# Expert products of a vision tower contracted over 128 + 64 rows instead of 96 + 96

## The reference

```python
# L0_ffn: W1 is 8 x 192 x 1024, W2 is 8 x 512 x 192
h = jnp.einsum('ecd,edh->ech', xg, W1)
act = h[..., :H] * jax.nn.silu(h[..., H:])
ye = jnp.einsum('ech,ehd->ecd', act, W2)
...
# L2_ffn: Wg and Wu are 16 x 768 x 192, Wd is 16 x 192 x 768
gate = jax.nn.silu(jnp.einsum('ecd,efd->ecf', xg, Wg))
up = jnp.einsum('ecd,efd->ecf', xg, Wu)
out = jnp.einsum('ecf,edf->ecd', gate * up, Wd)
```

## Time and profile before

| | us |
|---|---|
| median of 3 runs | 1151.77 |
| lowest, highest | 1146.94, 1162.23 |
| profiled execution | 1161.12 |
| span in its profile | 1159.3 |
| PE busy, share of the span | 77% |
| PE weight loads busy | 66% |
| DVE, ACT, POOL busy | 46%, 29%, 23% |

### The profile page before, as it was taken

The page is one execution under the profiler, slowest core; times in us unless marked ns, Lnnn a source line. Parts: engine busy times, 40 slices in busy tenths (PEclk is TensorE's granted clock), DMA queues, the critical chain, the costliest instruction groups (busy, mean ns, idle before and its releaser), DMA issues. The chain is left out here.

```text
span 1159.3 us, 31081 instructions
## 1 busy us (share of the span) xinstructions
PE 896.2 (77%) x13412; PEld 761.6 (66%) x13412; DVE 528.1 (46%) x1168; ACT 332.3 (29%) x677; POOL 261.9 (23%) x289
## 2 busy tenths in 40 slices
PE   8889986998369906899856795777779999387594
PEld 5578863886369905778755673655479999265472
DVE  1469963445343155554423365462821111464464
ACT  0247732212112202442442232333101212133132
POOL 1169840330134323210100101111033322200100
PEclk9989997778579967898876697785969999588598
DMA  7168757400458020000005100000438991100000
GB/s 211 29 142 184 177 154 227 102 1 1 136 168 222 23 63 1 2 3 1 2 1 139 47 4 1 2 3 27 124 83 208 259 222 14 30 3 1 2 4 23
DMA packets 58450, 88.29 MB, mean 76 GB/s; under 512 B 10756, under 2 KB 45000, under 8 KB 58340
## 3 DMA queue, kind: packets, MB, share of 16 engines
q1 hardware_dynamic: 53220, 81.85, 26.7%
q0 software_dynamic: 5120, 4.88, 2.2%
HBM read 78.30 MB, written 7.30 MB: 74 GB/s over the span
## 5 line engine op out<-in xcount | busy, mean ns | idle before, releaser
L2647 DVE TENSOR_TENSOR L_ffnhid<-L_ffnact_gate,L_ffnbank_u 128x300 f32<-128x300 f32 x32 | 15.0, 468 | 118.9 <-ACT L_ffnact_gate L2666 112.4
L1810 POOL TENSOR_SCALAR stage_hat_x<-stage_hat_x 128x320 f32<-128x320 f32 x40 | 51.2, 1280 | 20.4 <-ACT stage_hat_x L1786 20.4
L1720 PE MATMUL ps_places<-stage_own_y,stage_spread 80*64 80x128 f32 x800 | 54.8, 285 | 0.0
L1870 DVE TENSOR_TENSOR stage_product<-ps_rows,stage_hat_x 128x960 f32<-128x960 f32 x40 | 46.3, 1158 | 18.5 <-PE ps_rows L1731 15.2
L1731 PE MATMUL ps_rows<-stage_strip,stage_hat_y 64*32 64x96 f32 x3200 | 49.8, 256 | 6.3 <-DMA stage_strip<-in_strips 3.2
L1731 PEld LDWEIGHTS ps_rows<-stage_strip,stage_hat_y 64*32 64x32 f32 x3200 | 40.6, 108 | 13.4 <-issue 13.4
L1720 PEld LDWEIGHTS ps_places<-stage_own_y,stage_spread 80*64 80x64 f32 x800 | 44.9, 142 | 6.2 <-issue 0.8
L1110 PE MATMUL L_attnbank_q<-L_attnhT,L_attnwq 128*128 128x200 f32 x192 | 42.7, 369 | 6.9 <-DVE L_attnqT L1275 6.7
L2580 POOL DMA_INDIRECT stage_y_rows<-L_ffndown,stage_choice_index x16 | 25.4, 1589 | 90.4 <-ACT L_ffndown L2673 57.0
L1875 DVE TENSOR_REDUCE stage_samples<-stage_product 128x120 f32<-128x960 f32 x40 | 45.7, 1144 | 0.0
L1818 POOL TENSOR_TENSOR stage_hat_x<-stage_rel_x,stage_w_column 128x160 f32<-128x160 f32 x80 | 35.2, 461 | 45.8 <-POOLq L1522 45.8
(11 more groups left out here) (427 smaller groups left out, 2227.5 us busy)
## 6 DMA issues: line engine op xcount, KB each, us to landing
stage_strip<-in_strips SPq DMA_DIRECT2D x80, 189.0 KB, 3.6
L_ffn_win<-in_L_ffn_Win SPq DMA_DIRECT2D x10, 1152.0 KB
stage_L_ffn_win<-in_L_ffn_Win SPq DMA_DIRECT2D x6, 1152.0 KB
L_ffnranks<-stage_ranks SPq DMA_DIRECT2D x16, 400.0 KB
L_ffn_win<-in_L_ffn_Win SPq DMA_DIRECT2D x8, 768.0 KB
L_ffn_wout<-in_L_ffn_Wout SPq DMA_DIRECT2D x10, 576.0 KB
stage_L_ffn_wout<-in_L_ffn_Wout SPq DMA_DIRECT2D x6, 576.0 KB
L_ffn_wout<-in_L_ffn_W SPq DMA_DIRECT2D x8, 384.0 KB
```

Source lines behind the costliest of these rows:

```text
L1720: mm = nc.tensor.matmul(ps_places[HALF_P * h:HALF_P * (h + 1), p % 2, g * P:(g + 1) * P], k.spread[:, p * GRID + g, :], places[:, h * P:(h ...
L1810: nc.gpsimd.tensor_scalar(x, x, 1.0, 1.0, ALU.min, ALU.subtract).then_inc(s["hat_x"], 1)
L1870: nc.vector.tensor_tensor(products(i % 2), in_psum(i % 2), weights_x(i % BUFFERS), ALU.mult).then_inc(s["multiplied"], 1)
```

## The change

Channels are no longer split 96 + 96 but 128 + 64 (`REST` = 64). For each index tile f, gate and up are each one matmul over channels 0 to 127, and then one over channels 128 to 191. The rests of gate and up use different halves of PE's rows: gate rows 0 to 63, up rows 64 to 127. For this `win` gets a third block of columns, in which partitions 0 to 63 hold gate's last 64 channels and partitions 64 to 127 up's, laid out on the host; and `xT` holds the last 64 channels of the tokens twice, on both halves of the partitions. `turn` makes the second copy with a plain matmul by the identity whose output stands on partitions 64 to 127. The number of matmuls of `up` is the same, as is the order of its blocks; what `win` holds is as many bytes as before. Nothing else is changed.

```diff
-        xT = sb("xT", [HALF, 2, HALVES, 2 * C])
+        xT = sb("xT", [P, 2, 2, 2 * C])
...
-        ps_x = bank_x[0:HALF, :, 0:HALVES * 2 * C].rearrange("q b (k c) -> q b k c", k=HALVES)
+        ps_x = bank_x[:, :, 0:2 * 2 * C].rearrange("q b (k c) -> q b k c", k=2)
...
-                for h in range(HALVES):
-                    for k in range(2):
-                        mm = nc.tensor.transpose(ps_x[:, e % 2, h, k * C:(k + 1) * C], x[0:C, e, k, h * HALF:(h + 1) * HALF], tw.identity[0:C, 0:C])
+                for k in range(2):
+                    own = slice(k * C, (k + 1) * C)
+                    nc.tensor.transpose(ps_x[:, e % 2, 0, own], x[0:C, e, k, 0:P], tw.identity[0:C, 0:C])
+                    nc.tensor.transpose(ps_x[0:REST, e % 2, 1, own], x[0:C, e, k, P:DIM], tw.identity[0:C, 0:C])
+                    mm = nc.tensor.matmul(ps_x[REST:P, e % 2, 1, own], x[0:C, e, k, P:DIM], tw.identity[0:C, 0:C], start=True, stop=True)
...
                 for f in range(fb):
-                    for ps, at in ((ps_g, 0), (ps_u, hidden)):
-                        o = at + (c * fb + f) * P
-                        for k in range(HALVES):
-                            mm = nc.tensor.matmul(ps[:, c, f, :], weights.win[e % NB][:, k, o:o + P], xT[:, e % 2, k, :], start=(k == 0), stop=(k == 1))
+                    mm = weights.project_in(nc.tensor, e, c * fb + f, xT[:, e % 2], ps_g[:, c, f, :], ps_u[:, c, f, :])
...
-            self.win.append(tw.sb(f"{self.name}_win{b}", [HALF, HALVES, 2 * self.hidden]))
+            self.win.append(tw.sb(f"{self.name}_win{b}", [P, 3 * self.hidden]))
...
-        sp.dma_start(self.win[b][:], self.w_in[e].rearrange("(k q) n -> q k n", q=HALF)).then_inc(self.loaded[b], 16)
+        sp.dma_start(self.win[b][:], self.w_in[e]).then_inc(self.loaded[b], 16)
...
+    def project_in(self, pe, e, f, xT, gate, up):
+        w = self.win[e % len(self.win)]
+        low, high = slice(0, REST), slice(REST, P)
+        for ps, at in ((gate, 0), (up, self.hidden)):
+            pe.matmul(ps, w[:, at + f * P:at + (f + 1) * P], xT[:, 0, :], start=True, stop=False)
+        rest = slice(2 * self.hidden + f * P, 2 * self.hidden + (f + 1) * P)
+        pe.matmul(gate, w[low, rest], xT[low, 1, :], start=False, stop=True)
+        return pe.matmul(up, w[high, rest], xT[high, 1, :], start=False, stop=True)
```

More of the change, by code:

```diff
@@ L24 @@
 HALF = DIM // HALVES
+REST = DIM - P
 GROUPS = HEADS // 4
@@ L2544, in experts_by_row @@
         x = sb("x", [C, n_exp, DIM])
-        xT = sb("xT", [HALF, 2, HALVES, C])
+        xT = sb("xT", [P, 2, 2, C])
         act_gate = sb("act_gate", [P, 2, fb, C])
@@ L2549, in experts_by_row @@
         bank_x, bank_g, bank_u, bank_d = pb("bank_x"), pb("bank_g"), pb("bank_u"), pb("bank_d")
-        ps_x = bank_x[0:HALF, :, 0:HALVES * C].rearrange("q b (k c) -> q b k c", k=HALVES)
+        ps_x = bank_x[:, :, 0:2 * C].rearrange("q b (k c) -> q b k c", k=2)
         ps_g, ps_u = (b[:, :, 0:fb * C].rearrange("p b (f c) -> p b f c", f=fb) for b in (bank_g, bank_u))
@@ L2598, in turn @@
                     pe.wait_ge(s["xT_ready"], e - 1)
-                for k in range(HALVES):
-                    mm = nc.tensor.transpose(ps_x[:, e % 2, k, :], x[:, e, k * HALF:(k + 1) * HALF], tw.identity[0:C, 0:C])
+                nc.tensor.transpose(ps_x[:, e % 2, 0, :], x[:, e, 0:P], tw.identity[0:C, 0:C])
+                nc.tensor.transpose(ps_x[0:REST, e % 2, 1, :], x[:, e, P:DIM], tw.identity[0:C, 0:C])
+                mm = nc.tensor.matmul(ps_x[REST:P, e % 2, 1, :], x[:, e, P:DIM], tw.identity[0:C, 0:C], start=True, stop=True)
                 mm.then_inc(s["x_in_psum"], 1)
@@ L3140, in layout, with gate_and_up @@
     o["L0_ffn_Wg"] = a["L0_ffn_Wg"]
-    o["L0_ffn_Win"] = np.concatenate([a["L0_ffn_W1"][..., h:], a["L0_ffn_W1"][..., :h]], 2)
+    def gate_and_up(gate, up):
+        rest = np.concatenate([gate[:, P:], up[:, P:]], 1)
+        return np.concatenate([gate[:, :P], up[:, :P], rest], 2)
+    o["L0_ffn_Win"] = gate_and_up(a["L0_ffn_W1"][..., h:], a["L0_ffn_W1"][..., :h])
     o["L0_ffn_W2"] = a["L0_ffn_W2"]
     o["L2_ffn_gate"] = a["L2_ffn_gate_weight"].T
-    o["L2_ffn_Win"] = np.concatenate([a["L2_ffn_Wg"].transpose(0, 2, 1), a["L2_ffn_Wu"].transpose(0, 2, 1)], 2)
+    o["L2_ffn_Win"] = gate_and_up(a["L2_ffn_Wg"].transpose(0, 2, 1), a["L2_ffn_Wu"].transpose(0, 2, 1))
     o["L2_ffn_Wout"] = a["L2_ffn_Wd"].transpose(0, 2, 1)
```

## The result

| | before | after |
|---|---|---|
| median, us | 1156.95 | 1182.35 |
| lowest, highest | 1146.94, 1162.23 (4 runs) | 1179.41, 1186.32 (4 runs) |
| profiled execution, its span | 1161.12, 1159.3 | 1179.41, 1177.6 |

The ratio is 1.0221, with a 95% interval of 1.016 to 1.0283: 25 us slower. The forecast was 1180 and +28. That the kernel is slower is clear of the noise; that it is slower by more than 2%, the line that the forecast drew, is not.

A forecast was written before the change was run, and what follows sets the result against it. PE was taken to bound both expert stretches; index tiles +12.3 (stage 6) and +0.1 (stage 2), token transposes +16.6 and half clock -0.7 gave +28 us, 1180 against a median of 1151.8. Range 1162 to 1214 us, own range 1168 to 1192.

The forecast's parts named there:

- the line that the forecast drew: About 2% from the time before, at 1174.8 us, within which a measurement is not told from no change.
- What bounds: Expert stretches of stages 2 and 6: PE alone limits, so each nanosecond its queue gains or loses goes into the time.
- Halves side by side: 64-row rests of gate and up run together, starts 0.007 us apart; rival that they take turns, 1214 us, 11%.
- The price of a change: Each PE shape switch: 0.20 us plus 0.845 ns per moving column, 0.284 in stage 6, 0.403 in stage 2; no-drain rival 6%.
- The transposes: Token blocks: +0.49 us an expert in stage 6, +1.10 in stage 2, 16.6 in all; smaller-drain rival, 1169 us, 8%.
- Half clock: First 20 us of stage 6 and half of stage 2's first 11: together -0.7 us; large clock-falls rival, 1275 us, 6%.
- What costs nothing: Weight layout, transfers and wider token copies in the expert stages: no added time, as weights run ahead and ACT is idle.
- Sum: Whole kernel: 12.3 + 0.1 + 16.6 - 0.7 = +28 us, giving 1180 us against the median 1151.8.

The follow-up runs named there:

- experiment 3: Changed kernel with both rests on the low 64 rows of PE (up's values not the reference's): 1247.81 us, ratio to before 1.0791.
- Experiment 4: Changed kernel with the order inside every other index tile reversed, rests first, so one change of shape per tile instead of two: 1160.92 us, ratio to before 1.0064.
- experiment 2: Changed kernel with both rests contracted over all 128 rows, token block unchanged (values not the reference's): 1174.36 us, ratio to before 1.0174.
- Experiment 1: Changed kernel with the tokens' second copy made by transposes alone, no plain matmul left in the token block: 1173.97 us, ratio to before 1.0173.
- experiment 6: Kernel before with only `win` loaded as in the changed one, PE reading 96 rows (values not the reference's): 1155.79 us, ratio 0.9977.
- experiment 7: Changed kernel with rests over all 128 rows and the second token copy by transposes (values not the reference's): 1150.77 us, ratio to before 0.9949.
- experiment 11: Kernel of experiment 7 made to compute the reference, with zeros on the other operand's half of the moving tokens: 1154.38 us, ratio to before 0.9971.
- experiment 12: Kernel of experiment 11 with the rests of gate and up done in one matmul into one PSUM bank: 1148.65 us, ratio to before 0.9892.
- experiment 5: Changed kernel with every other tile's order reversed and the second token copy made by transposes alone: 1149.95 us, ratio to before 0.9925.
- 8: Kernel of experiment 7, unedited, run again for a second profile: 1152.45 us, ratio to before 0.9935.

## Why the prediction was right

- *What bounds.* PE alone, in both stretches, as forecast: they grew by 24.9 us and the time by 25.4. That the two agree this well is in part luck, since the time outside the stretches differs by up to 14 us from one execution to the next.
- *Halves side by side.* Right: a low and a high record start 0.007 apart, as forecast (they stand as 0.00 or 0.01 above), and forcing them to take turns costs 0.21 us a tile (experiment 3).
- *The price of a change.* 0.20 us plus the last columns: the forecast tile of stage 6, 1.02, is 1.017; stage 2's 1.625 is 1.613. Experiment 4 takes out one change for a tile and gets back 0.172 in stage 6 (0.284 - 0.112, to the digit), experiment 2 both.
- The Trainium skill (TensorEngine Tiling (Array Packing), Key Properties) says that changing the tiling mode drains TensorE. The trace agrees, and shows what it is worth here: 0.28 us with 100 columns, as much as two and a half records of stage 6.
- *The transposes.* Forecast +0.49 and +1.10 us for an expert, measured +0.49 (0.583 from first transpose to gate in place of 0.175, and the gate's own load exposed, 0.08) and +1.04 (1.35 in place of 0.41, and 0.10 for the load). Experiment 1 shows that the plain matmul is the cause.
- *Half clock.* Unchanged at 20 us in stage 6, by the rows of both profiles; a tile there is 1.78 us (857.05 to 858.83 in the timeline), 1.79 forecast.
- *What costs nothing.* Layout and wider copies: right (experiment 6 for the layout; experiment 7, whose tile is 0.894 and whose PE waits for a copy once, 0.5 us, as before, for both). That the transfers got lighter I had not seen.
- *Sum.* 28 forecast, 25 measured. The terms by the trace: tiles 0.123 x 96 = 11.8 less 0.009 x 32 = 0.3, tokens 7.8 + 8.3, together 27.6 at full clock. In the stretches it was 24.9: each begins behind its first token block (1.5 us), and at half clock a tile of stage 6 loses only 0.07 (1.78 against 1.71), 0.6 us over the first eleven. The median of before was 1151.8 when I forecast and 1157 to 1159 in the later runs, so the 1180 fell 5 short by its base and 3 over by its sum. That it lies 2 us from the measured 1182.35 is these two errors in part cancelling; the sum itself is right to a tenth.

## What to carry to other kernels

Count a switch between PE tile shapes as a lost weight load and an emptied pipe, here 0.28 us at 100 columns and full clock, and order the matmuls so that two groups of the same shape stand next to each other; look for it in the weight loads, since the matmul records show PE busy throughout. A transpose with a narrow output was free of it here, a plain matmul on the same tile was not. Where a half-empty contraction would need its own shape, zeros in the moving operand keep the shape; that alone was not told from no change here (experiment 11). Weights that two products share then need to be loaded only once, and with that the kernel was 1.1% faster than before (experiment 12), the reordered one 0.8% (experiment 5).

## What was not expected of the hardware

**When the clock rises.** The fourteen profiles of eleven kernels start stage 6 alike: the granted clock fell to 0.50 between 2.5 and 4.0 us before the first gate record. How long it stays there differs. Time at 0.50 from that record, worked out from PEclk in the windows (a window of 10 us at 0.77 has 4.6 us of it), by the rows of PE that the expert products use:

- All 128 rows always (experiments 7, 8, 11, 12): 4, 7, 6 and 4 us.
- 128 rows, but with the plain matmul in the token block (2): 13.
- 96 rows (before twice, 6): 20, 18, 17.
- 128 and paired 64 rows (after twice, 1, 4, 5): 20, 20, 20, 20, 17.
- 128 and single 64 rows (3): 24 to the rise, and 44 in all, with three more falls.

PE's records filled 9.5 to 10 of each 10 us in all of them, at a granted clock of 0.50 as at 1.00. The rows in use are one of several things that differ between these kernels: experiments 2 and 7 have the same index tiles and differ by the token block alone, and still by 6 to 9 us. None of the experiments sets the rows apart from the rest, so what decides the time at 0.50 stays open. In experiment 7 it was worth 8 us, 124.2 for stage 6 where 132.3 was worked out at the clock of before.

**Lighter transfers.** The same 1152 KB as 128 rows instead of 96 rows in two pieces keep the DMA engines busy a fifth less in 903:913 (0.83 against 1.04, at 247 and 249 GB/s) and 15% less in 883:893 (0.90 against 1.06, at 254 and 255). The experiment does not part the number of partitions from the size of the pieces.
